# First layer of a two-layer gated transformer on one core: the last norm step behind the next maximum, rows and statistics one batch further ahead, ScalarE's norms later in its slot

## The reference, cut to what matters

```
x = x + tanh(g_xattn[0]) * attention0(layernorm(x), ctx, ctx)   # 16 heads of 16
x = x + tanh(g_ffn[0])   * moe(layernorm(x))                    # 64 experts, top 8 in 4 of 8 groups
x = x + tanh(g_xattn[1]) * attention1(layernorm(x), ctx, ctx, mask)
x = x + tanh(g_ffn[1])   * quantised_ffn(layernorm(x))
layernorm(x) = (x - mean) / sqrt(var + 1e-5)                     # over the 256 features
```

## Time and profile before

| What | us |
|---|---|
| median of 3 runs | 1930.73 |
| the runs | 1928.98, 1930.73, 1933.91 |
| the profiled execution | 1926.39 |
| its span, first to last instruction | 1924.6 |
| PE busy in the span | 1731.2 (90%) |
| DVE busy | 1383.7 (72%) |
| ACT busy | 1178.2 (61%) |
| POOL busy | 611.8 (32%) |

### The profile page before, as it was taken

One profiled execution on the slowest core, in us unless ns is written; L12 is line 12 of the kernel. 1 busy time (PEld: TensorE's weight loads), 2 busy tenths in 40 slices (PEclk: granted clock), 3 DMA queues, 4 the chain that ended last, 5 costly groups with the idle time before them and its releaser, 6 DMA issues.

```text
span 1924.6 us, 54303 instructions
## 1 busy us (share of the span) xinstructions
PE 1731.2 (90%) x20208; PEld 1336.6 (69%) x20208; DVE 1383.7 (72%) x4587; ACT 1178.2 (61%) x2411; POOL 611.8 (32%) x616
## 2 busy tenths in 40 slices
PE   5999999999998299999999997599999999978855
PEld 4777777777777288888888886377777777743334
DVE  4888888888888456644444443488888888859988
ACT  3777777777776133332323222488888888858875
POOL 1000000000000146666666665322222222211147
PEclk9999999999999699999999999699999999989989
DMA  3222333222234568888778774332232323203265
GB/s 100 74 91 94 97 94 105 91 91 91 94 96 136 158 176 211 210 208 203 199 201 200 199 198 98 105 92 91 86 97 84 98 85 94 73 26 164 99 246 192
DMA packets 231349, 247.63 MB, mean 129 GB/s; under 512 B 29681, under 2 KB 207217, under 8 KB 228913
## 3 DMA queue, kind: packets, MB, share of 16 engines
q1 hardware_dynamic: 206272, 205.54, 33.1%
q0 software_dynamic: 24816, 38.62, 10.8%
HBM read 142.40 MB, written 101.66 MB: 127 GB/s over the span
## 4 chain that ended last, share of the span: by engine, by line
PE 47%; DVE 33%; ACT 7%; issue 6%; POOL 4%; SPq 1%; DMA 1%; POOLq 0%; DVEq 0%; ACTq 0%
DVE mt L800 15%; PE tiles L384 8%; PE bank L449 6%; ACT pt L582 6%; PE bank L1310 5%; PE tiles L1285 4%; PE tiles L367 4%; PE bank L1253 3%; PE tiles L351 3%; PE bank L479 3%; PE bank L1320 3%; DVE hmax L1731 3%; POOL rstd L1991 2%; PE bank L1297 2%; DVE h_ring L1724 2%
## 5 line engine op out<-in xcount | busy, mean ns | idle before, releaser
L1991 POOL TENSOR_TENSOR rstd<-var,minus_half 128x2 f32<-128x2 f32 x139 | 97.2, 699 | 736.5 <-DVE var L879 723.3
L800 DVE TENSOR_REDUCE mt<-tiles 128x16 f32<-128x2048 f32 x128 | 293.4, 2293 | 30.5 <-PE tiles L367 30.0
L582 ACT ACTIVATE pt<-tiles 128x2048 f32<-128x2048 f32 x128 | 240.7, 1881 | 49.1 <-PE tiles L384 49.1
L1516 POOL DMA_INDIRECT accumulator<-ye,tid x128 | 208.6, 1629 | 152.0 <-DVE ye L1449 132.2
L1449 DVE TENSOR_SCALAR ye<-bank,xr 128x256 f32<-128x256 f32 x128 | 56.0, 479 | 247.3 <-PE bank L1297 116.9
L384 PE MATMUL tiles<-qm,qkp 32*128 32x128 f32 x4096 | 151.1, 284 | 18.8 <-DVE mt L800 18.7
L384 PEld LDWEIGHTS tiles<-qm,qkp 32*128 32x128 f32 x4096 | 126.6, 187 | 48.3 <-DVE mt L800 33.7
L1501 POOL DMA_INDIRECT xr<-token_rows,tid x128 | 137.3, 1073 | 70.3 <-issue 38.5
L449 PE MATMUL bank<-xt,w_q 128*128 128x128 f32 x1024 | 154.8, 285 | 0.9 <-ACT xt L590 0.9
L367 PE MATMUL tiles<-qkp 32*128 32x256 f32 x2048 | 151.1, 408 | 3.3 <-ACT qkp L604 3.3
L449 PEld LDWEIGHTS bank<-xt,w_q 128*128 128x128 f32 x1024 | 131.8, 195 | 14.9 <-issue 13.3
(11 more groups left out here) (247 smaller groups left out, 4078.2 us busy)
## 6 DMA issues: line engine op xcount, KB each, us to landing
keys_values<-res SPq DMA_DIRECT2D x64, 256.0 KB
cxax<-accumulator SPq DMA_DIRECT2D x128, 128.0 KB, 2.2
cxax<-keys_values SPq DMA_DIRECT2D x128, 128.0 KB, 2.5
hidden_away<-h_ring SPq DMA_DIRECT2D x8, 1536.0 KB, 5.1
token_rows<-pay SPq DMA_DIRECT2D x64, 160.0 KB, 1.8
pt<-in_expert_up SPq DMA_DIRECT2D x36, 256.0 KB
cxax<-in_ctx SPq DMA_DIRECT2D x64, 128.0 KB, 2.2
res<-in_x SPq DMA_DIRECT2D x64, 128.0 KB, 2.3
```

The costliest lines, as they stand in the source:

```text
L582: nc.scalar.activation(pt[r % 2][:, :, :], tiles[:, :, :], ACT.Exp).then_inc(sem("exp_done"), 1)
L800: nc.vector.tensor_reduce(mt[:, :].rearrange("p (i n c) -> p i n c", i=RT, n=2 * KC)[:, :, :, 0], tiles[:, :, :].rearrange("p i (n k) -> p ...
L1516: nc.gpsimd.indirect_dma_start(out=acc[p][:, :], out_offset=bass.IndirectOffsetOnAxis(ap=tid[b % 8][:, h:h + 1], axis=0), in_=ye[r][:, h, ...
L1991: G.tensor_tensor(rstd[:, :], var[:, :], minus_half[:, :], ALU.pow).then_inc(sem(f"rstd_step_{L}"), 1)
```

## The change

In the first layer alone:

- `PAIR[0]` goes from 4 to 5 and `FIRST[0]`, the first slot, from -1 to -3. DVE's n becomes batch s+2, so statistics and variances of the first norm are taken one slot sooner. SP's `load` goes to stage(-3), one batch further ahead, and does nothing for batch 0.
- On DVE, step two of `inverses` (`nmr`) no longer ends the slot. The generator is kept in `pending`, and its last step runs in the next slot right after `maximum(m)`, and before `head_sums(o)`. `variances` now waits, in this layer too, until the step two of the pass before is done.
- On ACT, `normalise_first` leaves the head of the slot. `normalise_second(w)` goes behind `router_tanh(v)` and `copy_xt(f)`, and behind it stands `normalise_first(g)`, now of batch s+1, both before `copy_at(o)`.
- The small extra work of the first slots keeps its slots: its conditions go by stage(-1) instead of n.

```diff
-        PAIR = (4, 7)
+        PAIR = (5, 7)
...
-        FIRST = (-1, -3)
+        FIRST = (-3, -3)
...
                 if L == 0:
-                    normalise_first(f)
                     copy_counts(u)
                     copy_v(f)
-                    normalise_second(w)
                     router_tanh(v)
                     copy_xt(f)
+                    normalise_second(w)
+                    normalise_first(g)
                     copy_at(o)
...
             def variances(n, k):
-                if L == 1 and (n is not None or k is not None):
+                if n is not None or k is not None:
                     wait(dve, sm("rstd_step"), NORM_STEPS * (n[0] if n is not None else k[0] + PAIR[L]))
...
+            pending = []
+
             def body(stage):
                 m, o, w, v, u = (stage(lag) for lag in (1, 3, 4, 5, 6))
-                n = stage(-1 if L == 0 else -2)
+                n = stage(-2)
...
                 q = inverses(n, y)
+                last = pending.pop() if pending else None
+                if L == 0:
+                    pending.append(q)
...
                     maximum(m)
+                    if last is not None:
+                        next(last, None)
                     head_sums(o)
...
                     variances(n, y)
                     routing(1)
                     norming(1)
-                    routing(1)
-                    norming(1)
+                    routing(2)
...
-                if L == 0 and n is not None and n[0] == 0:
+                if L == 0 and stage(-1) is not None and stage(-1)[0] == 0:
                     spread_value_bias(dve, 0)
...
                 b, r = n
+                if b == 0:
+                    return
                 wait(sp, "v_done", first + b - 3)
                 wait(sp, "qk_done", first + b - 3)
...
-                    load(stage(-2))
+                    load(stage(-3))
```

More of the change, by code:

```diff
@@ L1034, in body @@
                     norming(1)
-                if L == 0 and n is not None and n[0] == 0:
+                if L == 0 and stage(-1) is not None and stage(-1)[0] == 0:
                     spread_value_bias(dve, 0)
-                if L == 0 and n is not None and n[0] == 1:
+                if L == 0 and stage(-1) is not None and stage(-1)[0] == 1:
                     split_biases(dve)
-                if L == 0 and n is not None and n[0] == 2:
+                if L == 0 and stage(-1) is not None and stage(-1)[0] == 2:
                     gate_scales()
```

## The result

The changed kernel took 1919.08 us (median of 4 runs, 1917.64 to 1920.65) against 1932.06 of the kernel before in the same comparison (1928.98 to 1933.91). The ratio is 0.9935 with a 95% interval of 0.9917 to 0.9952: faster by 0.65%, 12.6 us. Forecast were 1921.4 us and a gain of 9.3 us (ratio 0.9952), inside the range of 1914 to 1929, on the side forecast; the forecast ratio is the upper end of the measured interval, and the measured gain is the larger one. A second comparison of the same two kernels gave 0.9945 (0.9925 to 0.9966). The profiled execution took 1917.64 us with a span of 1915.9, 8.7 us less than before.

What follows compares the result with a forecast made beforehand. PE was taken as all but the bound, idling while DVE's maximum waited for POOL and `nmr`. Slots won 11.6 us, the end 0.8 and 0.9, the start lost 4.05: -9.25 us, 1921.4 us, range 1914 to 1929.

Steps and rivals of the forecast that it cites:

- The slot: Steady first-layer slots: the maximum no longer waits for POOL and `nmr`; 0.20 us gained each, 0.27 at most, 11.6 over 58.
- Rival 1: Steady slots: maximum starts earlier but another link keeps the slot at 0 to 0.10 us gain; 1927 to 1933 us, chance 0.20.
- What pays for it: DVE after the maximum: `nmr` takes 0.08 us there, covered by 0.27 us idle before the residual; added `variances` wait costs nothing.
- ACT: ACT's two norms move to its idle before `copy_at`; 0.41 us of slack in all, so the move costs nothing.
- Rival 3: ACT becomes the chain if norms end over 0.41 us later than worked out; 1938 us, 1975 at the far end, chance 0.08.
- SP: SP's load of a batch one slot earlier: the same two DMAs, a slot sooner, costing nothing.
- The start: Spreading the value bias waits for batch 1's rows, so PE starts at about 17.0 us: 4.05 us lost, 3.5 to 4.6.
- The clock: PE's half-clock fall near the start: same lost work, so zero, with 3 us either way if spared or longer.
- a half-clock stretch that is gone or twice as long: A sign near 35 us in the changed kernel's profile that the forecast sum is wrong.
- The end: Batch 62 and the drain: store goes out sooner, -0.8 us; tanh runs ahead of the second norm, -0.7 and -0.2.
- The sum: Whole kernel: 11.6 won in slots, 0.8 and 0.9 at the end, 4.05 lost at the start: -9.25 us, 1921.4 us.
- the likeliest case: Main case: slots gain 10.4 to 15.7 us, start costs 3.5 to 4.6, clock 3 either way; 1915 to 1927, chance 0.62.

Runs made afterwards that it cites:

- e2: Changed kernel with only `nmr` put back at the end of DVE's slot: 1936.68 us, ratio 1.0032 to the kernel before.
- e3: Changed kernel with ACT doing the first layer's first norm twice, once into a spare tile: 1921.39 us, ratio 0.9962 to the kernel before.
- e6: Changed kernel with ACT's two norms back at their former places (first norm at the slot's head, second behind the copy of the values): 2039.92 us, one run.
- e9: Changed kernel with only SP's load back to two batches ahead, `load(stage(-2))`: 1920.50 us, ratio 0.9956 to the kernel before.
- e1: Changed kernel with the value bias spread before batch 1's statistics again: 1914.02 us, ratio 0.9917 to the kernel before without one run of 6569.66 us.
- e4: Changed kernel with the value bias spread before the first slot, behind the scaling of the query weights: 1913.55 us, ratio 0.9923 to the kernel before.
- e5: e4 plus 8 extra PE matmuls behind the projections in the slots of batches 0 and 1: 1913.03 us, ratio 0.9910 to the kernel before.
- e0: The changed kernel repeated without any edit, against the kernel before: 1919.98 us, ratio 0.9945.
- e7: Kernel before with only `nmr` moved behind the next maximum, plus the wait in `variances` that it needs: 2028.52 us, one run.

## Why the prediction was right, step by step

- **The slot.** 0.20 us a slot from the hand-over in the earlier trace rows; measured 9.36 to 9.15 and 2.42 us from scores to `scores_t`. From batch 2 to 61 the sum is 12.7 us for 11.6; 59 slots count there, at 0.205 us, and the kernel before had two slots of 9.71 us that the changed one has not. Rival 1 is out.
- **What pays for it.** `nmr` behind the maximum takes the 0.08 us (305.14 to 305.21), and the residual still waits for PE, 17.0 / 60 = 0.28 us. The added wait was costed at nothing; it takes 0.07 us, hidden as the prediction said such a cost would be, and e2 shows it bare.
- **ACT.** Slack worked out 0.41 us, measured 0.43 (e3). Rival 3 needed norms that end over 0.41 us later than worked out; ACT was free for `copy_at` 1.33 us after `scores_t` started, where 1.37 was worked out. e6 shows what happens if the order is not changed.
- **SP.** Nothing, as forecast (e9).
- **The start.** The mechanism was right and the term a little too large: 3.20 us in place of 4.05, as batch 1's rows landed at 14.90 and not 15.78. In the repeated execution it was 3.86. It did not carry through whole, as the prediction had it: the first maximum came 2.70 us later in the one execution, 3.96 in the other. Taking it away brings 6 to 7 us by the medians (e1, e4, e5) and 2 to 7 by the ratios; whether that is more than PE's earlier start explains stays open.
- **The clock.** Taken as zero with 3 us either way. In the first execution the maximum of batch 2 shows 5.25 - 3.20 = +2.05 us, with two falls of about 6.8 us each; in the second one no fall came, and the same maximum shows 43.28 - 41.66 - 3.86 = -2.24. So both ends of the term came, each within its 3 us. But the prediction named a half-clock stretch that is gone or twice as long as a sign that its sum is wrong, and by that sign the term of zero held in neither execution. The Trainium skill ("TensorE: Matmul & The Clock Gate", Part 1) has windows that run freely, so that the same work can meet them differently; the two executions of one kernel, two falls and none, agree with it.
- **The end.** -1.7 forecast, -0.67 - 0.99 = -1.66 in the first trace. That it fits so well is luck. The tanh of batch 62 did run ahead of the norm, in both executions. But the step from batch 61 to 62, 11.45 us before, took 10.92 in the first execution and 12.90 in the second, and the drain from the last maximum to the experts, 45.81 before, took 44.82 and 46.11: by e0 the end costs 1.6 us. That the store goes out sooner and ACT waits less for it (2.25 us before) is not shown either: it waited 1.73 and 3.14.
- **The sum.** -9.25 forecast, -8.7 in the span of the first execution, where the slots won 1.1 more, the start with the clock cost 1.2 more and the stages behind gave 0.4 back: single errors of about 1 us that nearly cancel. The two medians give -13.0 and -10.2. The 1 to 4 us between can lie in the executions' own variation, which e0 shows to sit in several stages; which of them favours the changed kernel stays open. Two slips in the prediction's range change nothing here: the lower gain of the slots, 10.4 us (0.18 a slot), is worked out from no row, and the bounds of 1915 and 1927 for the likeliest case leave out the end; with its 1.7 us they are 1913.8 and 1926.2.

## What to carry to other kernels

In this kernel it paid to put a small cross-engine step (POOL's power and one DVE instruction, 0.66 us together) from the end of a software-pipelined slot behind the longest instruction of the next slot. But everything that reads its result had to go along, by one more batch ahead and a later place in the reader's queue: one part alone cost 98 us, the whole won 10 to 13. Look then at the first slot: work that hangs on a slot's number may now stand behind a load that it never needed. Spreading the bias before the slots brought the shortest kernels here, 1913 us (ratio 0.991 to 0.992), some 6 us less by the medians. Last, one execution's trace that agrees with a forecast term by term can do so by luck; a second execution of the same kernel shows which terms hold (here the slot does, the end does not).

## What the runs showed of the hardware that was not expected

- An added semaphore wait that had long been met cost DVE 0.07 us (0.53 against 0.46 us between the same two instructions; 0.52 in e7).
- The changed kernel's PE clock fell to half twice, for about 6.8 us each, in one execution, and not at all in the other; the maximum of batch 2 came 3.6 us later with the falls.
- At the start PE's first matmuls run slow whatever the granted clock says: the first four of `value_bias_out` take 2.04 us (0.51 each) with 1.00 in the rows of their stretch, where four of the same shape in `output` take 1.03. How long they stay slow differs from one execution to the next. Of the projections of batch 0 the second group took 0.61 us in the changed kernel's first execution and 1.06 in that of e9, again with 1.00 in the row; there only the fourth group, 8.2 us after PE's first matmul, was down to 0.71. The first maximum started 9.85 and 11.84 us after PE's first matmul. First the changed kernel, then e9:

```profile
21.54 0.61 PE L449 MATMUL bank<-cxax,w_k 128*128 128x128 f32 x4
```

```profile
22.95 1.06 PE L449 MATMUL bank<-cxax,w_k 128*128 128x128 f32 x4
...
22.00:24.00 2.00, 2.00 (x9) 2.00 (x10) 0.27 (x1) 0.38 (x1) 0.69 (x1) 1.00 0.00 0
```

- With PE idle for 1.5 us in each slot of 10.7 its clock fell to half in mostly every fourth slot (e6, e7); with 0.27 us or 0.07 us in a slot it fell in none between 60 and 580 us.
